# Attention heads: two 512-column score banks handled as one 1024-column tile, transposes grouped ahead of the weighings

## The reference

```
# q, k, v: (B, 16, 64, 8); mask depends on the layer (key mask, causal, or none)
scores = einsum("bhqd,bhkd->bhqk", q, k) / sqrt(8)
probs  = softmax(scores + mask, axis=-1)        # 64 keys
out    = einsum("bhqk,bhkd->bhqd", probs, v)    # then one 128x128 projection
```

## Time and profile before

| what | value |
|---|---|
| median of 3 runs | 1269.73 us (1269.73 to 1273.92) |
| the profiled execution | 1267.3 us |
| span of the profiled execution, first to last instruction | 1265.5 us |
| mean granted TensorE clock | 0.877 of full speed |
| busy share of PE, DVE, ACT, POOL | 86%, 53%, 37%, 27% |

### The profile page before, as it was taken

One profiled execution on the slowest core, in us unless ns is written; L12 is line 12 of the kernel. 1 busy time (PEld: TensorE's weight loads), 2 busy tenths in 40 slices (PEclk: granted clock), 3 DMA queues, 4 the chain that ended last, 5 costly groups with the idle time before them and its releaser, 6 DMA issues.

```text
span 1265.5 us, 25823 instructions
## 1 busy us (share of the span) xinstructions
PE 1084.6 (86%) x10082; PEld 915.3 (72%) x10082; DVE 676.5 (53%) x1560; ACT 463.2 (37%) x1005; POOL 338.2 (27%) x312
## 2 busy tenths in 40 slices
PE   5998988988799997979897887879699979889894
PEld 4666776766689987868576787757699957767783
DVE  3734745447566747372663646446565636355462
ACT  2634625426234333232341232325233345154231
POOL 1021035120251545121122410130432452341422
PEclk9998968989889996979896788889799989689697
DMA  9100001000152340000000100000022230010032
GB/s 340 43 1 1 2 1 52 2 1 2 25 181 71 85 175 16 2 1 1 1 2 7 44 2 1 1 1 2 19 77 82 62 127 15 1 35 2 30 91 73
DMA packets 54038, 52.99 MB, mean 42 GB/s; under 512 B 6816, under 2 KB 49312, under 8 KB 53024
## 3 DMA queue, kind: packets, MB, share of 16 engines
q1 hardware_dynamic: 48800, 40.85, 10.0%
q0 software_dynamic: 5120, 10.50, 2.9%
HBM read 34.02 MB, written 17.30 MB: 41 GB/s over the span
## 4 chain that ended last, share of the span: by engine, by line
PE 76%; DVE 11%; POOL 6%; issue 4%; ACT 2%; DMA 1%; SPq 1%; DVEq 0%; POOLq 0%
PE bank L1577 12%; PE bank L1589 7%; PE bank L509 5%; PE bank L498 5%; PE bank L327 5%; PE bank L290 4%; PE bank L873 3%; PE bank L307 3%; PE bank L485 3%; POOL small L365 2%; PE bank L836 2%; PE bank L318 2%; PE bank L476 2%; PE bank L911 2%; PE bank L894 2%
## 5 line engine op out<-in xcount | busy, mean ns | idle before, releaser
L365 POOL TENSOR_TENSOR small<-small,neghalf 128x4 f32<-128x4 f32 x56 | 56.5, 1018 | 501.1 <-DVE small L387 326.0
L1577 PE MATMUL bank<-xTs,qx 128*128 128x128 f32 x1160 | 160.9, 287 | 8.7 <-DVE qx L1648 5.0
L1577 PEld LDWEIGHTS bank<-xTs,qx 128*128 128x128 f32 x1160 | 144.7, 198 | 20.2 <-issue 15.6
L1263 POOL DMA_INDIRECT yg<-ybuf,posi x80 | 77.9, 973 | 180.8 <-DMA ybuf<-otx 153.9
L663 DVE TENSOR_REDUCE mx<-bank 128x8 f32<-128x512 f32 x128 | 88.1, 689 | 63.1 <-PE bank L485 60.9
L1589 PE MATMUL bank<-wmoe,otx 128*128 x764 | 106.8, 277 | 4.2 <-DVE otx L1677 2.7
L580 ACT ACTIVATE probsT<-bank 128x512 f32<-128x512 f32 x128 | 73.5, 597 | 84.9 <-PE bank L498 82.0
L498 PE MATMUL bank<-csb,probs 128*128 128x128 f32 x512 | 80.7, 289 | 22.9 <-ACT probs L584 22.9
L1589 PEld LDWEIGHTS bank<-wmoe,otx 128*128 128x128 f32 x764 | 95.1, 192 | 5.7 <-issue 5.3
L1237 POOL DMA_INDIRECT xbuf<-rows,posi x80 | 80.3, 1004 | 66.7 <-DVE ebi L1224 37.4
L290 PE MATMUL bank<-warm_x,warm_w 128*128 128x224 bf16 x588 | 97.2, 275 | 0.0
(11 more groups left out here) (266 smaller groups left out, 1976.6 us busy)
## 6 DMA issues: line engine op xcount, KB each, us to landing
ybuf<-otx SPq DMA_DIRECT2D x122, 64.0 KB
xblk<-xbuf SPq DMA_DIRECT2D x26, 256.0 KB
wmoe<-in_w_moe SPq DMA_DIRECT2D x3, 2048.0 KB, 10.0
wmoe<-in_w_moe SPq DMA_DIRECT2D x1, 3072.0 KB, 11.6
xbuf<-otx SPq DMA_DIRECT2D x2, 1472.0 KB, 20.4
wmoe<-in_w_moe SPq DMA_DIRECT2D x1, 1536.0 KB, 14.8
xbuf<-rows,posi POOLq DMA_INDIRECT x80, 2.2
yg<-ybuf,posi POOLq DMA_INDIRECT x80
```

Source lines behind the costliest of these rows:

```text
L365: g.tensor_tensor(s.col(1)[:, at:at + PC], s.col(0)[:, at:at + PC], neghalf[:, 0:PC], ALU.pow)\
L1263: nc.gpsimd.indirect_dma_start(yg[:, p % 2, k, i, :], None, ybuf[g].ap(), bass.IndirectOffsetOnAxis(ap=posi[g][:, j:j + 1], axis=0)).then_ ...
L1577: mm = pe.matmul(U[half][:, ch * P:(ch + 1) * P], w[:, 0:P], xTs[:, na % 3, :], start=True, stop=True)
```

## The change

The two banks of a stream that hold scores become one tile of 1024 columns, `both_scores`. For each stream and round DVE now makes one maximum and one subtraction over 1024 columns, and ACT one exponential over 1024. On PE the order of the last four slots of a round becomes: transposes of the even unit, transposes of the odd unit, weighing of the even unit, weighing of the odd unit, all of the round before. Both transposes still go to the one bank `TP`, so the second waits until ACT has copied the first out. The subtraction waits until both transposes of the round before have read `probs`, of which there is one copy for a stream. `normed_context` moves from the last slot of rounds 2 and 4 to the slot of the subtraction in rounds 3 and 4, ahead of the subtraction. `keep_warm` runs three times in one slot of rounds 1, 2 and 4, where it ran 1, 2 and 3 times in three slots.

```diff
-WARM_CENTRE, WARM_MEAN, WARM_PROJ, WARM_HEADS = 4, 4, 3, (1, 2, 3)
+WARM_CENTRE, WARM_MEAN, WARM_PROJ, WARM_HEADS = 4, 4, 3, 3
...
-        banks = [ctx.enter_context(nc.psum_tensor(f"bank{i}", [P, W2T], F32)) for i in range(8)]
+        bank_pairs = [ctx.enter_context(nc.psum_tensor(f"banks{i}", [P, 2 * W2T], F32)) for i in range(4)]
+        banks = [bank_pairs[i // 2][:, i % 2 * W2T:(i % 2 + 1) * W2T] for i in range(8)]
...
+                self.both_scores = bank_pairs[2 * i]
...
@@ heads_pe @@
                 else:
                     pe.wait_ge(*c.next("shifted"))
-                    pe.wait_ge(*c.next("shifted"))
...
             def transposes(k):
-                pe.wait_ge(*c.next("exped"))
+                if k % 2 == 0:
+                    pe.wait_ge(*c.next("exped"))
+                else:
+                    pe.wait_ge(*c.next("probsT_taken"))
...
             def weigh(k):
-                pe.wait_ge(*c.next("probsT_taken"))
+                if k % 2 == 1:
+                    pe.wait_ge(*c.next("probsT_taken"))
...
                 if j >= 1:
-                    weigh(2 * j - 2)
+                    transposes(2 * j - 2)
                 yield
                 if j >= 1:
                     transposes(2 * j - 1)
-                    keep_warm(s, WARM_HEADS[0])
+                    if j != 3:
+                        keep_warm(s, WARM_HEADS)
                 yield
                 if j >= 1:
-                    keep_warm(s, WARM_HEADS[1])
+                    weigh(2 * j - 2)
+                yield
+                if j >= 1:
                     weigh(2 * j - 1)
                 yield
-                if j < ROUNDS:
-                    transposes(2 * j)
-                    if j != 2:
-                        keep_warm(s, WARM_HEADS[2])
-                yield
-            c.skip("shifted", 2)
+            c.skip("shifted")
...
@@ heads_act @@
             for j in range(ROUNDS + 1):
-                if j >= 1:
-                    exped(2 * j - 1)
                 yield from idle(4)
                 if j >= 1:
+                    taken(2 * j - 2)
+                yield
+                if j >= 1:
                     taken(2 * j - 1)
                 yield
                 if j < ROUNDS:
-                    exped(2 * j)
-                yield
-                if j < ROUNDS:
-                    taken(2 * j)
+                    a.wait_ge(*c.next("shifted"))
+                    a.activation(s.squares, s.squares, ACT.Exp).then_inc(*c.give("exped"))
                 yield
...
@@ heads_dve @@
+            tops = s.mx[:, :, :].rearrange("p u a -> p (u a)")
             for j in range(ROUNDS + 1):
-                yield from idle(2)
+                yield from idle(3)
                 if j < ROUNDS:
-                    maximum(2 * j)
-                yield
-                if j < ROUNDS:
-                    shifted(2 * j)
-                yield
-                if j < ROUNDS:
-                    maximum(2 * j + 1)
-                yield
-                if j < ROUNDS:
-                    shifted(2 * j + 1)
-                yield
-                if j in (2, 4):
-                    normed_context(j // 2 - 1)
+                    dve.wait_ge(*c.next("scores"))
+                    dve.wait_ge(*c.next("scores"))
+                    link(c, dve.tensor_reduce(tops, by_head(s.both_scores[:, :]), AX.X, ALU.max))
+                yield
+                if j in (3, 4):
+                    normed_context(j - 3)
+                if j < ROUNDS:
+                    if j >= 1:
+                        dve.wait_ge(*c.next("probsT"))
+                        dve.wait_ge(*c.next("probsT"))
+                    dve.tensor_tensor(by_head(s.squares), by_head(s.both_scores[:, :]),
+                                      tops.unsqueeze(2).to_broadcast([P, 16, SEQ]), ALU.subtract)\
+                       .then_inc(*c.give("shifted"))
+                yield
+                yield
                 yield
```

More of the change, by code:

```diff
@@ L520, in heads_pe @@
                 if j >= 1:
+                    transposes(2 * j - 2)
+                yield
+                if j >= 1:
+                    transposes(2 * j - 1)
+                    if j != 3:
+                        keep_warm(s, WARM_HEADS)
+                yield
+                if j >= 1:
                     weigh(2 * j - 2)
@@ L523, in heads_pe @@
                 if j >= 1:
-                    transposes(2 * j - 1)
-                    keep_warm(s, WARM_HEADS[0])
-                yield
-                if j >= 1:
-                    keep_warm(s, WARM_HEADS[1])
                     weigh(2 * j - 1)
                 yield
-                if j < ROUNDS:
-                    transposes(2 * j)
-                    if j != 2:
-                        keep_warm(s, WARM_HEADS[2])
-                yield
-            c.skip("shifted", 2)
+            c.skip("shifted")
             pe.wait_ge(*c.next("context_normed"))
@@ L580, in taken @@
                 a.activation(s.probsT[:, k % 2, :], s.TP[:, :], ACT.Copy).then_inc(*c.give("probsT_taken"))
-            def exped(k):
-                a.wait_ge(*c.next("shifted"))
-                a.activation(s.probs[:, k % 2, :], s.probs[:, k % 2, :], ACT.Exp).then_inc(*c.give("exped"))
             for j in range(ROUNDS + 1):
+                yield from idle(4)
                 if j >= 1:
-                    exped(2 * j - 1)
-                yield from idle(4)
+                    taken(2 * j - 2)
+                yield
                 if j >= 1:
```

## The result

The changed kernel takes 1303.78 us (median of 4 runs, 1302.3 to 1309.79) against 1269.73 before (four runs as well, 1268.28 to 1273.92): the ratio is 1.0272, 95% interval 1.023 to 1.0313. The forecast had the sign, but 1283 with a range up to 1298: it saw 13 us of some 34. The profiled execution of the changed kernel took 1304.98 us, its span is 1302.9.

The account below looks back on a forecast made before the run. TensorE was taken to fill the third round, VectorE's chain to be the path in round four. Six masked stages at +1.81 us and two unmasked at +1.26 gave +13.4, so 1283 us, range 1265 to 1298.

Parts of the forecast that it names:

- the prices of the 1024-column operations: For operations over both banks: a maximum or a subtraction takes 1.22 us, an exponential 1.04 us.
- the first round: Masked stage, first mask to next mask: 6.11 us against 7.50, so -1.39.
- the third round with the wait on `TP` paid for by fewer fillers: Masked stage: 7.04 us against 7.02, as the fillers taken out pay for the wait on the one transpose bank.
- the second round at full clock: Masked stage: the parts sum to 7.69 us, before any loss to the lower clock.
- The divisions: Round four: each stream's moved `normed_context`, 0.78 us, stands before its subtraction on VectorE's chain, which is the path.
- In an unmasked stage the first round: Without 0.96 us of masks, the first round takes 5.15 us against 6.99, so -1.84.
- The last part at full clock with the moved divisions: Masked stage, round four to the stage's last division: 15.27 us against 12.50, so +2.77.
- Theory B: Posed for the follow-up runs: the schedule itself is longer than worked out, at any clock.
- the second round's sum: Masked stage: 7.69 us plus 0.76 lost by mask b at the lower clock, 8.45 against 8.04, so +0.41.
- the sum of the fourth round: Masked stage: VectorE's chain ends at 8.65 us, exponential b at 9.77, the last division at 15.27.
- a second stretch at the lower clock: Rival: longer TensorE waits bring a further 3.4 us at 0.50, losing 1.7 a stage, 13.6 in all: 1297; chance 0.15.

Follow-up runs that it names:

- e2_fill_first: The changed kernel with 18 more fillers of each stream in TensorE's first wait of a stage: 1294.37 us, ratio 1.0194 to the kernel before.
- e3_norm_fill: The changed kernel with the first tile's `normed_context` back in round two's last slot and 18 more fillers of each stream in TensorE's first wait: 1271.71 us.
- e6_before_fill: The kernel before the change with 10 more fillers of each stream in TensorE's first wait of a stage: 1261.24 us, ratio 0.9923.
- e8_before_lean: The kernel before the change with 1, 1 and 0 fillers instead of 1, 2 and 3 in a round's three slots: 1271.42 us, ratio 1.0004.

## Why the prediction was wrong

Right were the prices of the 1024-column operations and, in a masked stage, the first round, the third round with the wait on `TP` paid for by fewer fillers, and the second round at full clock (7.69 forecast, 7.64 in e2_fill_first). The divisions did stand in VectorE's chain. In an unmasked stage the first round was mis-sized, 6.26 us for 5.15, since the forecast let stream a's scores go ahead without subtraction b; the second round is shorter for it, 6.27 at full clock where 6.95 was forecast without its 0.5 for the clock, and the third is 6.26 for 6.08. That is 0.6 us a stage too little. The last part at full clock with the moved divisions was in no run; e2_fill_first has 16.25 with a clock of 0.89, and such a stretch cost 1.47 in e3_norm_fill, so an estimate is 16.25 - 1.47 = 14.8, against 15.27 forecast. With the divisions put back it is 13.62; the forecast less their 1.56 is 13.7. Theory B fell: the sums, where the clock is 1.00, are right within a few tenths of a microsecond a round in a masked stage.

The step that failed is the clock: in the second round's sum, "if the lower clock holds until the same moment", and in the sum of the fourth round, where no term for the clock stood. In a masked stage the forecast counted 0.76 us of it. The size of that term is an estimate, as the last parts are: the changed stage is 6.02 + 7.64 + 6.94 + 14.8 = 35.4 at full clock and took 40.03, so 4.6. Before, the same difference is 35.06 - 34.12 (e6_before_fill) = 0.9. Of the 5.0 us that the first masked stage lost, 3.7 are clock and 1.3 are schedule. For the first unmasked stage, with 6.26 + 6.27 + 6.26 (the distances from scores to scores in e2_fill_first) and 14.0 for the last part (15.42 at a clock of 0.89 in the second unmasked stage of e2_fill_first, less 1.47), 32.8 for 35.41, it is 2.6 against 0.4 and a schedule of 1.5. Scaled to eight stages the clock is 6 x 3.7 + 2 x 2.2 = 26.6 us and the schedule 6 x 1.3 + 2 x 1.5 = 10.8, in all 37.4, where 38.2 were measured. The stages lost between 3.7 and 5.9 us each, and how the loss of a rotary stage divides is not shown, as no run has one at full clock in the old order. The 13 us forecast are close to the schedule, in part by luck: the last part was put 0.5 us too long in a masked stage, and the unmasked rounds 0.6 too short.

The rival "a second stretch at the lower clock" named the mechanism and both its places. It allowed for one further stretch of 3.4 us a stage and gave it 1.7 us and a chance of 0.15, though both waits pointed to one each, and the first masked stage had an estimated 10 us more at 0.50. It should have been part of the likeliest case: the first wait grew by 40%, the divisions were known to stop TensorE twice, and the earlier trace rows showed what 2.85 us of waiting does. A second slip hides behind the first: the last part was worked out along VectorE's chain at TensorE's full speed, but at 0.50 TensorE's own list is the longer path.

What stays open: how the longer second-round stretch divides between the longer wait (4.00 us) and the fewer fillers behind it. e8_before_lean shows that fewer fillers alone can lengthen it, e2_fill_first that covering the wait removes it; no run has the long wait with the old number of fillers. Fillers in the waits of round four while the divisions stand there were not tried: they write the bank that the divisions read. Why the rest of the program takes 978 us in one run and 992 in another is open too.

## What to carry to other kernels

Work out a reordered schedule twice, at the full clock and with TensorE at 0.50 behind every wait that the new order makes; a wait that costs 1 us in the chain can cost as much again behind it (1.47 us behind waits of 0.62 and 0.48 in e3_norm_fill). Before merging operations to save their fixed part, look at who waits while the longer one runs, and do not move work into the one list that sets the path just because a slot is free there. If TensorE's wait can't be removed, filling it with small matmuls cost nothing here (the first round takes 6.02 us with them and 6.01 without) and was worth 0.8%, to the old kernel as to the new.

## What the runs showed of the hardware

TensorE can be held at 0.50 while it is busy without a break: 10.39 of 10.39 us in e8_before_lean. Waits as short as 0.62 and 0.48 us were followed by the lower clock in some stages and not in others of the same program (15.09 and 13.62 us for the same work). Two VectorE operations of 512 columns without a wait between them start 0.60 us apart at 0.69 us each, so that joining two maxima into one saved some 0.06 us (0.60 + 0.68 against 1.22), not the 0.16 by which 1.22 is less than twice 0.69. A maximum over 1024 columns in two PSUM banks took 1.225 us, where 512 columns in one bank took 0.689.
